# A Perceiver layer's cross-attention: the scores of a step's second 128 queries are issued after the first two turnings of probabilities

## The chip, the cores and the metric

The kernel runs on one core of one Trainium2 chip. The metric is device time in microseconds for one execution of the whole program. A core has a matrix engine (PE, with its weight loads listed apart as PEld), a vector engine (DVE), an activation engine (ACT), a general engine (POOL) and a queue for DMAs (SP). Each works through its own list of instructions in the order in which the program wrote them, and they meet through semaphores.

## What is computed

One layer of a Perceiver: x (2 x 256 x 256) attends to a context (2 x 4096 x 256) with 16 heads of 64, then come a self-attention and a gated feed-forward part with quantized weights. The change concerns the cross-attention alone:

```python
q = (scale * (Q @ Wq + bq)).reshape(bs, q_len, NH, DM)
k = (K @ Wk + bk).reshape(bs, kv_len, NH, DM)
v = (V @ Wv + bv).reshape(bs, kv_len, NH, DM)
qk = jnp.einsum('nlhd,nshd->nhls', q, k)
a = jax.nn.softmax(qk, axis=-1)
o = jnp.einsum('nhls,nshd->nlhd', a, v).reshape(bs, q_len, NH * DM)
return o @ Wo + bo
```

Q is the normalized x, K and V are both the context.

## The kernel before

The cross-attention is cut into 128 steps, n = 0 to 127. A step is one head (h), 1,024 of the 4,096 keys (chunk c) and all 256 queries of one batch, held as two halves of 128 (qt = 0 and 1). Sixteen steps (four chunks by four heads) make a group g, with k = n % 16; there are eight groups. Products are taken in a high and a low part for exactness, hence the names with hi and lo.

The matrix engine's list for step n is: the scores of the next step, n + 1 (`scores`, L292 to L305: for each half of the queries six matmuls with 64 rows, two at a time in the upper and lower half of the array, into that half's own two banks of `psS`); the wait of `bank_free` (L440 to L447), which holds the engine until the shared bank `psW` may be written again; in some steps one piece of other work into `psW`; two turnings of step n's probabilities (`turn`, four 128x128 transposes each, into `psT`); the projection of keys that will be needed four steps later (`project_k`, L341, into `psW`); the third and fourth turning; the products with the values (`values`, L329 and L330) with the projection of values (`project_v`, L354, into `psW`) between them. `project_k` has a wait of its own (L464 to L472) where the other work of the step has still to be read out of `psW`.

The other work depends on k. Steps with k = 1 to 7 of groups 1 to 7 turn outputs of the group before (`post`, L378), which DVE weighs (L667) out of `psW`; so does k = 0, where DVE first works out the weights (L652 to L659). Step k = 8 turns the summed outputs (`turn_o`, L386), k = 9 projects them (`project_o`, L395). Steps with k = 12 to 15 project queries of the next group (`project_q`, L365), which ACT (L533) and DVE (L630) read. Steps with k = 10 and 11 have nothing. Steps 0 to 7 and 48 to 63 also turn a piece of the context at their end (`turn_ctx`, L371) into `psW`, which ACT copies (L538) and DVE subtracts (L636, semaphore `prep_l`); the `bank_free` of the following step waits for that.

DVE's list in a step is: the maximum over the first half of the next step's scores (L613), the other work, `p_low` for the first two turnings (L619), the maximum over the second half, the sum of a weighed output (L676) if there is one, `p_low` for the last two, and the low part of the values (L624). ACT's list is: `p_high` twice (L544), the exponential of the first half (L510), the copy of the projected keys (L520), `p_high` twice, the exponential of the second half, the copies of values (L527) and outputs (L603). The order in which each engine's work is written out is the only thing that sets it; no planner is involved. The last four steps project no keys or values any more.

Of the kernel before, what the change touches and what calls it, by code (L numbers as in the profile page):

```python
# [14 lines left out]
def cross_attention(nc, x, ctx, Wq, bq, Wk, bk, Wv, bv, Wo, ident, y):  # L15
# [6 lines left out]
    QT = S // P  # L22
# [9 lines left out]
    N = GP * STEPS  # L32
# [12 lines left out]
    with ExitStack() as st:  # L45
# [79 lines left out]
        def wait(eng, s, val):  # L125
            if val > 0:
                eng.wait_ge(s, val)

        def place(n):

            return n // STEPS, n % STEPS // GH, n % GH

        def prep_unit(n):


            if n < 8:
                return 8 + n
            if (GP // 2 - 1) * STEPS <= n < GP // 2 * STEPS:
                return 2 * NP + n - (GP // 2 - 1) * STEPS
            return None  # L140
# [6 lines left out]
        def prob_slot(n, qt):  # L147
            return (2 * n + qt) % 3
# [140 lines left out]
        def _(pe):  # L289
            mm = pe.matmul  # L290

            def scores(n):  # L292
                g, c, h = place(n)
                if n % 2 == 0:
                    wait(pe, k_split, 4 * (n + 2))
                if c == 0:
                    wait(pe, q_ok, GH * g + h + 1)
                for qt in range(QT):
                    wait(pe, exp_ok, 2 * (n - 1) + qt + 1)
                    for i, (q, part) in enumerate(((q_hi, 0), (q_lo, 0), (q_hi, 1))):  # L300
                        for half in range(2):
                            rows = slice(HD * half, HD * half + HD)
                            last = mm(psS[:, qt, half * PIECE:(half + 1) * PIECE], q[rows, h, qt * P:(qt + 1) * P],  # L303
                                      kT[rows, n // 2 % KRING, h % 2, part, :], start=(i == 0), stop=(i == 2))
                    last.then_inc(s_ok, 1)  # L305

            def turn(n, t):
                if t == 0:
                    wait(pe, exp_ok, 2 * n + 2)
                wait(pe, pl_ok, 4 * n + t - 1)  # L310
                for k in range(2):
                    for qt in range(QT):
                        last = pe.transpose(psT[:, t % 2, k * S + qt * P:k * S + qt * P + P],  # L313
                                            prob[:, prob_slot(n, qt), (2 * t + k) * P:(2 * t + k + 1) * P],
                                            ident[:, :])
                last.then_inc(t_ok, 1)

            def values(n, t):
                h = n % GH
                unit = n // GH * GH + t  # L320
                wait(pe, pl_ok, 4 * n + t + 1)
                if t == 0:
                    wait(pe, oc_ok, n)
                if h == 0:
                    wait(pe, v_lo, unit + 1)
                for k in range(2):
                    w = v[:, unit % VRING, k, h, :, :].rearrange("p a d -> p (a d)")
                    at = (4 * n + t) % PRING
                    mm(psO[:, 0:S], w, pT_hi[:, at, k * S:(k + 1) * S], start=(t == 0 and k == 0), stop=False)  # L329
                    last = mm(psO[:, 0:S], w, pT_lo[:, at, k * S:(k + 1) * S], start=False,  # L330
                              stop=(t == TB - 1 and k == 1))
                last.then_inc(av_ok, 1)

            def project_k(m, dst):
                g, c, i = place(m)
                if m % STEPS == 0:
                    wait(pe, wk_ok, 2 * g + 2)
                piece = 2 * c + i % 2
                for j, (a, x_) in enumerate(((0, ctxT_hi), (1, ctxT_hi), (0, ctxT_lo))):
                    for kt in range(KT):  # L340
                        last = mm(dst, wk_s[:, a, kt, i // 2 * P:(i // 2 + 1) * P],  # L341
                                  x_[:, kt, piece * PIECE:(piece + 1) * PIECE],
                                  start=(j == 0 and kt == 0), stop=(j == 2 and kt == KT - 1))
                last.then_inc(k_ps, 1)
# [13 lines left out]
            def project_q(g, h, dst):  # L358
                if h == 0:
                    wait(pe, wq_ok, 8 * g + 8)  # L360
                b = g // QUADS
                for j, (a, x_) in enumerate(((0, xnT_hi), (1, xnT_hi), (0, xnT_lo))):
                    for kt in range(KT):
                        twin = wq_s[:, a, kt, h, :, :].rearrange("p a d -> p (a d)")
                        last = mm(dst, twin, x_[:, kt, b * S:(b + 1) * S],  # L365
                                  start=(j == 0 and kt == 0), stop=(j == 2 and kt == KT - 1))
                last.then_inc(q_ps, 1)
# [6 lines left out]
            def post(g, k, dst):  # L374
                h, qt = k // QT, k % QT
                wait(pe, oc_ok, STEPS * g + 12 + h + 1)
                for c in range(NCH):
                    last = pe.transpose(dst[:, c * P:(c + 1) * P], oT[:, h, out_slot(g, c), qt * P:(qt + 1) * P],  # L378
                                        ident[:, :])
                last.then_inc(post_ps, 1)  # L380

            def turn_o(g):
                wait(pe, comb, 16 * (g + 1))
                for half in range(2):
                    for qt in range(QT):
                        last = pe.transpose(psW[:, half * S + qt * P:half * S + (qt + 1) * P],  # L386
                                            on[:, qt, half * P:(half + 1) * P], ident[:, :])
                last.then_inc(o2_ps, 1)

            def project_o(g):  # L390
                wait(pe, wo_in, 16 * (g + 1))
                wait(pe, o2_ok, 2 * (g + 1))
                for qt in range(QT):
                    for half in range(2):
                        last = mm(psW[:, qt * D:(qt + 1) * D], o2T[:, half, qt * P:(qt + 1) * P], wo[:, half, :],  # L395
                                  start=(half == 0), stop=(half == 1))
                last.then_inc(y_ps, 1)
# [42 lines left out]
            def bank_free(n):  # L440

                if n == 0:
                    pe.wait_ge(q_ok, GH)
                elif prep_unit(n - 1) is not None:
                    wait(pe, prep_l, prep_unit(n - 1) + 1)
                else:
                    wait(pe, v_lo, min(n + LEAD, N))  # L447

            for n in range(N):
                g, k = n // STEPS, n % STEPS  # L450
                if n + 1 < N:
                    scores(n + 1)
                bank_free(n)
                if k < 8 and g >= 1:
                    post(g - 1, k, psW[:, :])
                elif k == 8 and g >= 1:
                    turn_o(g - 1)
                elif k == 9 and g >= 1:
                    project_o(g - 1)
                elif k >= 12 and g + 1 < GP:  # L460
                    project_q(g + 1, k - 12, psW[:, 0:S])
                turn(n, 0)
                turn(n, 1)
                if n + LEAD < N:  # L464
                    if k < 8 and g >= 1:
                        wait(pe, comb, 16 * (g - 1) + 2 * k + 1)
                    elif k == 8 and g >= 1:
                        wait(pe, o2_ok, 2 * g)
                    elif k == 9 and g >= 1:
                        wait(pe, y_ok, g)  # L470
                    elif k >= 12 and g + 1 < GP:
                        wait(pe, q_ok, GH * (g + 1) + k - 12 + 1)  # L472
                    project_k(n + LEAD, psW[:, :])
                turn(n, 2)
                turn(n, 3)
                early = prep_unit(n) is not None
                values(n, 0)
                if not early:
                    values(n, 1)
                if n + LEAD < N:  # L480
                    wait(pe, kraw_ok, n + LEAD + 1)
                    project_v(n + LEAD, psW[:, :])
                if early:
                    values(n, 1)
                values(n, 2)
                values(n, 3)
                u = prep_unit(n)
                if u is not None:
                    wait(pe, cst_in, 16 * (u // KT - FIRST + 1))
                    wait(pe, v_lo, n + LEAD + 1)  # L490
                    turn_ctx(u, cst, psW[:, :])
# [912 lines left out]
```

## Time and profile before

| | us |
|---|---|
| median of 3 runs | 1438.99 |
| lowest and highest | 1438.51, 1441.53 |
| the profiled execution | 1441.08 |
| its span in the trace | 1439.4 |
| PE busy | 1336.4 (93%) |
| DVE busy | 1025.7 (71%) |
| ACT busy | 882.1 (61%) |
| POOL busy | 621.7 (43%) |

The profiled execution took 1.7 us more than the span that its instructions cover. The scores of the cross-attention are computed from 42.6 us to 1200.8 us of the span, so the change touches four fifths of it. The records of a matmul overlap, since matmuls are pipelined; what counts here is where one matmul or weight load starts after the one before it.

### The profile page before, as it was taken

How to read it: one execution, taken by the hardware profiler on the slowest of the kernel's cores; microseconds unless marked ns; L12 is line 12 of the kernel's file. 1: busy time of each engine (PE TensorE's matmuls, PEld its weight loads, DVE VectorE, ACT ScalarE, POOL GpSimd, SP SyncE). 2: the span in 40 equal slices, each digit the busy share in tenths (PEclk: the TensorE clock that was granted, in tenths of full speed). 3: DMA queues.
4: the chain of work that ended last, by engine and by line, in shares of the span. 5: the costliest groups of instructions: out<-in, count | busy, mean ns of one | idle time of the engine just before them, and what ended most of it. 6: DMA issues, size and time to landing. Idle time of an engine off the chain costs nothing. (4 is left out here: it accounts for less than half of the span.)

```text
span 1439.4 us, 24781 instructions
## 1 busy us (share of the span) xinstructions
PE 1336.4 (93%) x9380; PEld 1136.4 (79%) x9380; DVE 1025.7 (71%) x1407; ACT 882.1 (61%) x1716; POOL 621.7 (43%) x749
## 2 busy tenths in 40 slices
PE   5899999999999999999999999999999997489857
PEld 4788888888888888888888888888888885267734
DVE  3666678767876786678766876687668867389666
ACT  2667666666666666766666666666666664256511
POOL 5355546454645454535454555455554440000000
PEclk9999999999999999999999999999999999589979
DMA  4010000000000010100000000000000000300000
GB/s 124 16 45 2 15 1 9 8 16 1 8 9 31 2 36 30 38 30 1 9 23 1 2 8 23 1 1 8 8 1 2 1 8 1 99 0 1 1 1 15
DMA packets 25940, 22.95 MB, mean 16 GB/s; under 512 B 5472, under 2 KB 25568, under 8 KB 25824
## 3 DMA queue, kind: packets, MB, share of 16 engines
q1 hardware_dynamic: 25824, 21.39, 5.0%
q8 instruction: 75, 1.23, 0.4%
q14 instruction: 41, 0.34, 0.1%
HBM read 20.86 MB, written 0.52 MB: 15 GB/s over the span
## 5 line engine op out<-in xcount | busy, mean ns | idle before, releaser
L544 ACT ACTIVATE pT_hi<-psT 128x512 fp32r<-128x512 f32 x512 | 293.1, 600 | 219.6 <-PE psT L313 199.2
L619 DVE TENSOR_TENSOR pT_lo<-psT,pT_hi 128x512 fp32r<-128x512 f32 x512 | 332.5, 685 | 81.6 <-ACT pT_hi L544 75.8
L613 DVE TENSOR_REDUCE negm<-psS 128x1 f32<-128x1024 f32 x256 | 311.7, 1218 | 52.3 <-PE psS L303 52.3
L264 POOL TENSOR_TENSOR kT<-kraw,khi 64x512 fp32r<-64x512 f32 x252 | 325.0, 1290 | 0.0
L258 POOL CAST khi<-kraw 128x512 fp32r<-128x512 f32 x126 | 76.9, 610 | 510.3 <-ACT kraw L520 509.5
L510 ACT ACTIVATE prob<-psS,negm 128x1024 f32<-128x1024 f32 x256 | 285.5, 1115 | 1.0 <-DVE negm L613 1.0
L313 PE MATMUL psT<-ident,prob 128*128 128x128 f32 x2048 | 268.5, 274 | 3.9 <-DVE pT_lo L619 3.9
L329 PE MATMUL psO<-pT_hi,v 128*128 128x256 f32 x1024 | 267.5, 294 | 1.2 <-DVE pT_lo L619 0.4
L313 PEld LDWEIGHTS psT<-ident,prob 128*128 128x128 f32 x2048 | 234.3, 141 | 34.0 <-issue 7.1
L330 PE MATMUL psO<-pT_lo,v 128*128 128x256 f32 x1024 | 255.7, 282 | 0.0
L303 PE MATMUL psS<-kT,q_hi 64*128 64x512 f32 x1024 | 194.6, 416 | 3.4 <-ACT prob L510 2.0
L329 PEld LDWEIGHTS psO<-pT_hi,v 128*128 128x128 f32 x1024 | 195.4, 191 | 2.7 <-DVE pT_lo L619 2.6
L330 PEld LDWEIGHTS psO<-pT_lo,v 128*128 128x128 f32 x1024 | 196.0, 191 | 0.0
L624 DVE TENSOR_TENSOR v<-psW,v 128x512 fp32r<-128x512 f32 x125 | 86.4, 691 | 115.7 <-ACT v L527 115.7
L354 PE MATMUL psW<-wv_s,ctxT_hi 128*128 128x256 f32 x1000 | 160.6, 283 | 0.0
L263 POOL CAST kT<-kraw 64x512 fp32r<-64x512 f32 x252 | 153.4, 609 | 15.6
L341 PE MATMUL psW<-ctxT_hi,wk_s 128*128 128x512 f32 x496 | 148.6, 421 | 10.7 <-DVE q_lo L630 5.9
L354 PEld LDWEIGHTS psW<-wv_s,ctxT_hi 128*128 128x128 f32 x1000 | 137.9, 192 | 0.1
L303 PEld LDWEIGHTS psS<-kT,q_hi 64*128 64x128 f32 x1024 | 96.2, 184 | 39.4 <-issue 6.4
L341 PEld LDWEIGHTS psW<-ctxT_hi,wk_s 128*128 128x128 f32 x496 | 83.8, 189 | 41.1 <-DVE q_lo L630 12.6
L303 PE MATMUL psS<-kT,q_lo 64*128 64x512 f32 x512 | 101.4, 393 | 0.0
L354 PE MATMUL psW<-wv_s,ctxT_lo 128*128 128x256 f32 x500 | 100.7, 283 | 0.0
(213 smaller groups left out, 1590.6 us busy)
## 6 DMA issues: line engine op xcount, KB each, us to landing
cst<-in_ctx_dram SPq DMA_DIRECT2D x12, 512.0 KB, 3.9
oT<-in_ctx_dram SPq DMA_DIRECT2D x4, 512.0 KB, 5.0
wraw<-in_L_xattn_Wk_dram SPq DMA_DIRECT2D x8, 256.0 KB, 2.6
wraw<-in_L_xattn_Wv_dram SPq DMA_DIRECT2D x8, 256.0 KB, 3.4
wraw<-in_L_xattn_Wq_dram SPq DMA_DIRECT2D x8, 256.0 KB, 2.6
wo<-in_L_xattn_Wo_dram SPq DMA_DIRECT2D x8, 256.0 KB, 2.7
ff_wdn<-in_L_ffn_w_down_dram SPq DMA_DIRECT2D x1, 704.0 KB, 8.7
ff_win<-in_L_ffn_w_gate_dram SPq DMA_DIRECT2D x1, 640.0 KB, 6.0
```

The source lines that it names most:

```text
L263: pool.tensor_copy(kT[half, m // 2 % KRING, h, 0, :], raw[own, :]).then_inc(k_split, 1)
L264: pool.tensor_tensor(kT[half, m // 2 % KRING, h, 1, :], raw[own, :], khi[own, :].bitcast(F32), ALU.subtract).then_inc(k_split, 1)
L303: last = mm(psS[:, qt, half * PIECE:(half + 1) * PIECE], q[rows, h, qt * P:(qt + 1) * P], kT[rows, n // 2 % KRING, h % 2, part, :], start= ...
L313: last = pe.transpose(psT[:, t % 2, k * S + qt * P:k * S + qt * P + P], prob[:, prob_slot(n, qt), (2 * t + k) * P:(2 * t + k + 1) * P], id ...
L329: mm(psO[:, 0:S], w, pT_hi[:, at, k * S:(k + 1) * S], start=(t == 0 and k == 0), stop=False)
L330: last = mm(psO[:, 0:S], w, pT_lo[:, at, k * S:(k + 1) * S], start=False, stop=(t == TB - 1 and k == 1))
L341: last = mm(dst, wk_s[:, a, kt, i // 2 * P:(i // 2 + 1) * P], x_[:, kt, piece * PIECE:(piece + 1) * PIECE], start=(j == 0 and kt == 0), st ...
L354: last = mm(dst[:, k * GD:(k + 1) * GD], x_[:, kt, keys], wv_s[:, a, kt, :], start=(j == 0 and kt == 0), stop=(j == 2 and kt == KT - 1))
L510: act.activation(prob[:, prob_slot(n, qt), :], psS[:, qt, :], ACT.Exp, bias=negm[:, g % 2, h, qt, c:c + 1], accum_out=lsum[:, g % 2, h, qt ...
L544: act.activation(pT_hi[:, i % PRING, :], psT[:, t % 2, :], ACT.Copy).then_inc(ph_ok, 1)
L613: dve.tensor_reduce(negm[:, g % 2, h, qt, c:c + 1], psS[:, qt, :], AX.X, ALU.max, negate=True)\
L619: dve.tensor_tensor(pT_lo[:, i % PRING, :], psT[:, t % 2, :], pT_hi[:, i % PRING, :].bitcast(F32), ALU.subtract).then_inc(pl_ok, 1)
```

## The change

`scores` takes a list of halves. A step calls it for the first half of the queries where it stood before, and for the second half after the second turning, ahead of `project_k` and of the wait in front of it. Nothing else is changed, on any engine; matmuls, tiles and semaphores are the same ones.

```diff
--- before.py
+++ after.py
@@ -289,13 +289,13 @@
         def _(pe):
             mm = pe.matmul
 
-            def scores(n):
+            def scores(n, qts=(0, 1)):
                 g, c, h = place(n)
                 if n % 2 == 0:
                     wait(pe, k_split, 4 * (n + 2))
                 if c == 0:
                     wait(pe, q_ok, GH * g + h + 1)
-                for qt in range(QT):
+                for qt in qts:
                     wait(pe, exp_ok, 2 * (n - 1) + qt + 1)
                     for i, (q, part) in enumerate(((q_hi, 0), (q_lo, 0), (q_hi, 1))):
                         for half in range(2):
@@ -449,7 +449,7 @@
             for n in range(N):
                 g, k = n // STEPS, n % STEPS
                 if n + 1 < N:
-                    scores(n + 1)
+                    scores(n + 1, (0,))
                 bank_free(n)
                 if k < 8 and g >= 1:
                     post(g - 1, k, psW[:, :])
@@ -461,6 +461,8 @@
                     project_q(g + 1, k - 12, psW[:, 0:S])
                 turn(n, 0)
                 turn(n, 1)
+                if n + 1 < N:
+                    scores(n + 1, (1,))
                 if n + LEAD < N:
                     if k < 8 and g >= 1:
                         wait(pe, comb, 16 * (g - 1) + 2 * k + 1)
```

On PE, at the start of step 1, a step without other work that follows one with a turned piece of context. `psS` holds scores, `psT` turned probabilities, `psW` is the shared bank; `exp_ok` says that an exponential has been taken, `pl_ok` that a turning has been read, `prep_l` that a context piece has left `psW`. Before:

```order
L303 MATMUL psS<-kT,q_hi 128x512
L303 MATMUL psS<-kT,q_lo 128x512 x2
L303 MATMUL psS<-kT,q_hi 128x512 x2
L303 MATMUL psS<-kT,q_hi 128x512 [waits exp_ok]
L303 MATMUL psS<-kT,q_hi 128x512
L303 MATMUL psS<-kT,q_lo 128x512 x2
L303 MATMUL psS<-kT,q_hi 128x512 x2
L313 MATMUL psT<-ident,prob 128x128 [waits pl_ok,exp_ok,prep_l]
L313 MATMUL psT<-ident,prob 128x128 x3
L313 MATMUL psT<-ident,prob 128x128 [waits pl_ok]
L313 MATMUL psT<-ident,prob 128x128 x3
L341 MATMUL psW<-ctxT_hi,wk_s 128x512 x4
```

After:

```order
L303 MATMUL psS<-kT,q_hi 128x512
L303 MATMUL psS<-kT,q_lo 128x512 x2
L303 MATMUL psS<-kT,q_hi 128x512 x2
L313 MATMUL psT<-ident,prob 128x128 [waits pl_ok,exp_ok,prep_l]
L313 MATMUL psT<-ident,prob 128x128 x3
L313 MATMUL psT<-ident,prob 128x128 [waits pl_ok]
L313 MATMUL psT<-ident,prob 128x128 x3
L303 MATMUL psS<-kT,q_hi 128x512 [waits exp_ok,q_ok,k_split]
L303 MATMUL psS<-kT,q_hi 128x512
L303 MATMUL psS<-kT,q_lo 128x512 x2
L303 MATMUL psS<-kT,q_hi 128x512 x2
L341 MATMUL psW<-ctxT_hi,wk_s 128x512 x4
```

The second half's six matmuls (four rows) moved behind eight transposes, and the transposes, with their wait for `prep_l`, moved up by those six.

On PE again, in step 13, which projects queries (L365) whose reading out of `psW` (`q_ok`) the first matmul of L341 waits for. Before:

```order
L303 MATMUL psS<-kT,q_hi 128x512 [waits exp_ok]
L303 MATMUL psS<-kT,q_hi 128x512
L303 MATMUL psS<-kT,q_lo 128x512 x2
L303 MATMUL psS<-kT,q_hi 128x512 x2
L365 MATMUL psW<-xnT_hi,wq_s 128x256 [waits v_lo]
L365 MATMUL psW<-xnT_hi,wq_s 128x256 x3
L365 MATMUL psW<-xnT_lo,wq_s 128x256 x2
L313 MATMUL psT<-ident,prob 128x128 [waits pl_ok,exp_ok]
L313 MATMUL psT<-ident,prob 128x128 x3
L313 MATMUL psT<-ident,prob 128x128 [waits pl_ok]
L313 MATMUL psT<-ident,prob 128x128 x3
L341 MATMUL psW<-ctxT_hi,wk_s 128x512 [waits q_ok]
```

After:

```order
L365 MATMUL psW<-xnT_hi,wq_s 128x256 [waits v_lo]
L365 MATMUL psW<-xnT_hi,wq_s 128x256 x3
L365 MATMUL psW<-xnT_lo,wq_s 128x256 x2
L313 MATMUL psT<-ident,prob 128x128 [waits pl_ok,exp_ok]
L313 MATMUL psT<-ident,prob 128x128 x3
L313 MATMUL psT<-ident,prob 128x128 [waits pl_ok]
L313 MATMUL psT<-ident,prob 128x128 x3
L303 MATMUL psS<-kT,q_hi 128x512 [waits exp_ok,k_split]
L303 MATMUL psS<-kT,q_hi 128x512
L303 MATMUL psS<-kT,q_lo 128x512 x2
L303 MATMUL psS<-kT,q_hi 128x512 x2
L341 MATMUL psW<-ctxT_hi,wk_s 128x512 [waits q_ok]
```

Here the second half's scores now stand between the turnings and the matmul that waits for `q_ok`; the projection of queries follows the first half's scores directly.

## Rows read from the trace of the kernel before

**Rows 1.** Windows: stretch, length, busy us (instructions) by engine, PE clock, DMA, GB/s.
```profile
787.00:1190.00 403.00, 398.28 (x2946) 345.90 (x2944) 301.90 (x389) 270.62 (x507) 208.58 (x246) 1.00 0.02 6
```
**Rows 2.** Timeline of a step without other work: start, length, engine, line, work.
```profile
740.84 0.28 PE L330 MATMUL psO<-pT_lo,v 128*128 128x256 f32 x1
741.04 0.18 PEld L303 LDWEIGHTS psS<-kT,q_hi 64*128 64x128 f32 x2
...
741.15 0.19 PEld L303 LDWEIGHTS psS<-kT,q_lo 64*128 64x128 f32 x2
741.38 0.40 PE L303 MATMUL psS<-kT,q_lo 64*128 64x512 f32 x2
...
742.31 0.39 PE L303 MATMUL psS<-kT,q_hi 64*128 64x512 f32 x2
742.63 0.85 PEld L313 LDWEIGHTS psT<-ident,prob 128*128 128x128 f32 x8 [0.36 <-issue]
...
743.45 0.76 PEld L341 LDWEIGHTS psW<-ctxT_hi,wk_s 128*128 128x128 f32 x4
...
749.27 0.50 PE L303 MATMUL psS<-kT,q_hi 64*128 64x512 f32 x2
```
**Rows 3.** Timeline of a step that turns outputs, PE and DVE.
```profile
704.61 0.69 DVE L624 TENSOR_TENSOR v<-psW,v 128x512 fp32r<-128x512 f32 x1 [0.68 <-ACT v L527]
...
704.83 0.50 PE L303 MATMUL psS<-kT,q_hi 64*128 64x512 f32 x2
...
705.84 1.23 DVE L613 TENSOR_REDUCE negm<-psS 128x1 f32<-128x1024 f32 x1 [0.53 <-PE psS L303]
...
706.91 1.04 PE L313 MATMUL psT<-ident,prob 128*128 128x128 f32 x8
...
707.11 0.69 DVE L667 TENSOR_TENSOR oweighed<-psW,wts 128x512 f32<-128x512 f32 x1
...
707.85 1.20 PE L341 MATMUL psW<-ctxT_hi,wk_s 128*128 128x512 f32 x4
```
**Rows 4.** Timeline of a group's first step, where DVE works out weights beforehand.
```profile
790.78 0.50 PE L341 MATMUL psW<-ctxT_hi,wk_s 128*128 128x512 f32 x1 [0.57 <-DVE oweighed L667]
```
**Rows 5.** Timeline of a step that projects queries.
```profile
758.74 0.50 PE L303 MATMUL psS<-kT,q_hi 64*128 64x512 f32 x2
...
760.33 0.53 PEld L365 LDWEIGHTS psW<-xnT_hi,wq_s 128*128 128x128 f32 x4 [0.36 <-issue]
...
761.14 1.03 PE L313 MATMUL psT<-ident,prob 128*128 128x128 f32 x8
761.34 0.47 ACT L533 ACTIVATE q_hi<-psW,bqT 128x256 fp32r<-128x256 f32 x1 [2.10 <-PE psW L365]
...
761.85 0.48 DVE L630 SCALAR_TENSOR_TENSOR q_lo<-psW,bqT,q_hi 128x256 fp32r<-128x256 f32 x1 [0.87 <-ACT q_hi L533]
762.38 0.30 PEld L341 LDWEIGHTS psW<-ctxT_hi,wk_s 128*128 128x128 f32 x2 [0.45 <-DVE q_lo L630]
```
**Rows 6.** Timeline after a turned piece of context: a step without other work.
```profile
591.45 0.63 PE L371 MATMUL psW<-ident,cst 128*128 128x128 f32 x4 [0.28 <-DVE v L624]
592.00 0.19 PEld L303 LDWEIGHTS psS<-kT,q_hi 64*128 64x128 f32 x2 [0.17 <-issue]
...
592.74 0.69 DVE L636 TENSOR_TENSOR ctxT_lo<-psW,ctxT_hi 128x512 fp32r<-128x512 f32 x1 [1.44 <-ACT ctxT_hi L538]
...
593.59 0.85 PEld L313 LDWEIGHTS psT<-ident,prob 128*128 128x128 f32 x8 [0.36 <-DVE ctxT_lo L636]
...
594.41 0.77 PEld L341 LDWEIGHTS psW<-ctxT_hi,wk_s 128*128 128x128 f32 x4
```
**Rows 7.** The same after a turned piece, in a step that turns outputs.
```profile
502.08 0.19 PEld L303 LDWEIGHTS psS<-kT,q_hi 64*128 64x128 f32 x2 [0.17 <-issue]
...
505.29 0.30 PEld L341 LDWEIGHTS psW<-ctxT_hi,wk_s 128*128 128x128 f32 x2 [0.34 <-DVE oweighed L667]
```
**Rows 8.** Timeline of step 124, the first without projections.
```profile
1184.41 0.50 PE L303 MATMUL psS<-kT,q_hi 64*128 64x512 f32 x2
...
1187.32 1.29 DVE L619 TENSOR_TENSOR pT_lo<-psT,pT_hi 128x512 fp32r<-128x512 f32 x2 [0.68 <-ACT pT_hi L544]
...
1190.39 0.39 PE L329 MATMUL psO<-pT_hi,v 128*128 128x256 f32 x1
```

## Prediction

> **What bounds the kernel now.** I read the share of busy time by stretch first. Over 403 us of steps PE has work in flight for 398 us, at the full granted clock, with DVE at 302 and ACT at 271 [rows 1]. So PE sets the pace, and the question is what its list costs in another order. For that I read the timeline of one step of each kind, by starts. The reader is to see two sorts of lost PE time: places where the array is not fed although nothing is waited for, and places where PE waits before the projection of keys (L341).
>
> The first sort stands at both edges of the block of scores [rows 2]. The last value matmul starts at 740.84; inside that block they follow each other every 0.12, so the array is free at 740.96, yet the scores' first weight load starts at 741.04: 0.08 lost. The second pair's load starts at 741.15, so the first load held things up for 0.11 with no matmul to cover it. Then pairs start every 0.23 (the second at 741.38, the last at 742.31), and the last one leaves the array free at 742.54, but the transposes' load starts at 742.63: 0.09 lost. The whole block takes 1.59 from its first load to the next work's. Loads of other work don't show this: from the transposes to L341 it is 743.45 right at the end of eight starts of 0.11. The same 1.59 stands before L365 [rows 5], and when the scores follow transposes of the context (591.45 to 592.00 for four, where four need 0.44 and the first one's load 0.05) about 0.06 is again lost at entry [rows 6]. What differs at all these edges is that scores use 64 rows of the array and everything else 128.
>
> **What the change adds.** A second block of three pairs, between transposes and L341: 0.08 at entry, 0.11 for its first load, 0.09 at its exit, and 0.11 for the first load of L341, now without cover. That is **0.39 a step** if PE waits for nothing. One block of three pairs takes 1.59 - 3 x 0.23 = 0.90 to the next work's load. I take 0.39 from these rows; the bounds are 0.34 and 0.44 (the entry at 0.06 rather than 0.08 and the uncovered load of L341 a little shorter, against a longer exit).
>
> The Trainium skill (TensorEngine Tiling (Array Packing), Key Properties) says that changing the tiling mode drains the engine. The gaps of 0.08 and 0.09 agree with that; the two uncovered loads are more than the sentence says.
>
> **What it removes**, by kind of step. Times in brackets count from the step's first load of scores. In the new order other work starts at 0.90, the turnings after it, they take 0.87 (eight starts of 0.11; 0.92 when they come straight after scores), the second block starts 0.08 later, and L341's load 0.90 after that.
>
> - Steps with nothing else, 15 and the opening one: no wait before L341 to cover, so +0.39 each: **+6.2**.
> - Steps that turn outputs [rows 3]: L341 waits for the weighing, which ends at 707.80, and starts at (3.02). The weighing follows the maximum of the first half, 705.84 to 707.07, which doesn't move. In the new order the turnings start at (1.39) instead of 706.91 (2.08), end at (2.26), and L341 can start at (2.34 + 0.90 = 3.24). So the wait vanishes and +0.22 is left. There are 42 of them outside the stretch below, and six steps with the output projection, whose L341 waits about as long: 48 x 0.22 = **+10.5**. The six that turn summed outputs wait a little longer: **+0.4** together.
> - The first step of a group [rows 4]: the weighing is released at 3.68 after the start, later than 3.24, so L341 starts as before: **0**, six times.
> - Steps that project queries [rows 5]: L341 waits for the low part of the queries until 762.38 (3.64). In the new order they are projected at (0.90) instead of 760.33; their reading ends at about (2.9), set by DVE's maximum; turnings run (1.71) to (2.58), and L341 can start at (3.56): -0.08 each, 24 times: **-2.0**.
> - The last three steps with scores [rows 8]: no L341 follows, and the chain of readings binds. The second maximum starts after the readings of the first two turnings, 1187.32 to 1188.61, and the values' third part waits until 1190.39. Turnings that start 0.69 earlier move the chain by about 0.65, since the first maximum ends at (2.24) and lets the readings start at (2.27) rather than 1187.32 (2.91): **-2.0** together.
>
> **What it uncovers.** After a step that ended with a turned piece of context, the bank is busy until DVE has read it at 592.74 + 0.69 = 593.43 (1.43), and the turnings wait for that [rows 6]. Before, 1.59 of scores hid it fully: the load starts at 593.59, right when scores end. With 0.90 of scores it is not hidden, and PE waits 0.58 until (1.48). It gets back only 0.11 of its former 1.59. For the ten such steps without other work the turnings then end at (2.40), and L341's load starts at (3.38) instead of 594.41 (2.41), its matmul 0.01 later still: +0.98, **+9.8**. Four such steps project queries: from (1.48) the sum gives (4.14) instead of (3.64): **+2.0**. Ten have other work; for those that turn outputs it gives 1.48 + 0.49 + 0.87 + 0.08 + 0.90 = (3.82) instead of 505.29 (3.21) [rows 7]: about +0.61, **+6.2**.
>
> All waits of other engines behind this have room. DVE's second maximum finds its scores about 1.0 after the block's start, (3.4) in a step that turns outputs, while its own reading of the turnings keeps it busy until (4.2). The bank is free of values at 705.30 (0.47) [rows 3], before the (0.90) at which other work wants it. The third and fourth turning come later than before while what they wait for comes earlier. POOL's split keys and the DMAs are asked for at the same places of the list.
>
> **The sum:** 6.2 + 10.5 + 0.4 - 2.0 - 2.0 + 9.8 + 2.0 + 6.2 = **+31.1 us**. On the profiled execution's own 1441.1 (span 1439.4 and 1.7 around it) that is 1472.2; it lies 2.1 above the median of 1438.99, so against the median I say **1470.1**. With 0.05 more or less for a change of tiling in some 118 steps: 1464 to 1476.
>
> **Rivals.**
>
> 1. *The changes of tiling cost nothing in the new place.* For it: the transposes are short, and weight loads elsewhere hide. Against: the entry from context transposes and the exits above. With 0 instead of 0.39, the plain steps cost nothing, those that turn outputs stay at the weighing, the 24 with queries gain 0.47 each (-11.3), the last three 2.0, and the uncovered steps still add 10 x 0.59, 4 x 0.11 and 10 x 0.22: 8.5. Sum -4.8: **1434**, on the faster side. It decides from about 0.07 a step downwards.
> 2. *The drain is paid but both loads are hidden*: 0.17 a step. 16 x 0.17 - 24 x 0.30 - 2.0 + 10 x 0.76 + 4 x 0.28 + 10 x 0.39 = +6: **1445**. The Trainium skill (TensorE: Matmul & The Clock Gate, Step-by-step: what each phase is for) has the engine pull weight loads ahead of running matmuls when row groups don't conflict or a background buffer is used; by that rule this is the outcome. Inside a block of scores the trace agrees, at its edges it doesn't.
> 3. *The uncovering does not happen*, because the piece of context is read sooner than DVE's row shows: 24 x 0.58 = 14 less, **1456**.
> 4. *The waits aren't covered*: if what releases L341 moves along with it, all 127 steps pay 0.39 and the uncovering comes on top: 49.5 + 14 = +64, **1503**. Against it: the maximum of the first half, which sets the weighing, stays.
> 5. *No effect*, because the engine would take matmuls in another order than written: **1439**.
>
> **Chances.** Forecast 0.76, rival 1 0.04, rival 2 0.05, rival 3 0.05, rival 4 0.08, rival 5 0.02. The range reaches down to rival 3 and, with the forecast's own bounds and a few us by which the clock may fall differently in the part after the steps, up to 1484: **1456 to 1484**. A measurement can tell about 0.2% (3 us) from no change. Faster: 0.04; within 0.2%: 0.03 (rival 5 and a share of the others' edges); slower: 0.93.
>
> **What would show it.** In the new profile: a plain step of 8.62 instead of 749.27 - 741.04 = 8.23; two blocks of three pairs of scores, each 0.90 to the next load; no wait of L341 for L667 or L630 except at a group's first step; steps of about 10.1 after a turned piece, with PE waiting about 0.58 for L636 before the turnings. Blocks of 0.7 would point to rivals 1 and 2; a PE wait for L619 or L510, or DVE's second maximum idle for scores, would mean that a chain I called loose is not.

## The result and the profile after

The changed kernel takes 1472.97 us (median of 4 runs, 1471.44 to 1474.92); the kernel before, measured again beside it, 1440.26. The ratio is 1.0221, with a 95% interval of 1.0189 to 1.0253: slower by about 32 us. Forecast were 1470.1 us and 31.1 us more. The span grew from 1439.4 to 1469.7 us.

The page shows why shares of busy time don't help here: PE is busy for 93% before and after.

```profile
span 1469.7 us, 24860 instructions
...
PE 1364.8 (93%) x9380; PEld 1126.9 (77%) x9380; DVE 1029.4 (70%) x1407; ACT 892.2 (61%) x1716; POOL 621.7 (42%) x749
```

Lines behind the added call are two higher in the new kernel (L613 is L615, L636 is L638, L667 is L669). The timeline of a step without other work, which answers to [rows 2]:

```profile
766.91 0.28 PE L330 MATMUL psO<-pT_lo,v 128*128 128x256 f32 x1
767.12 0.19 PEld L303 LDWEIGHTS psS<-kT,q_hi 64*128 64x128 f32 x2
...
767.69 0.39 PE L303 MATMUL psS<-kT,q_hi 64*128 64x512 f32 x2
768.01 0.86 PEld L313 LDWEIGHTS psT<-ident,prob 128*128 128x128 f32 x8 [0.36 <-DVE v L626]
...
769.03 0.19 PEld L303 LDWEIGHTS psS<-kT,q_hi 64*128 64x128 f32 x2 [0.17 <-issue]
...
769.14 0.19 PEld L303 LDWEIGHTS psS<-kT,q_lo 64*128 64x128 f32 x2
...
769.60 0.40 PE L303 MATMUL psS<-kT,q_hi 64*128 64x512 f32 x2
...
769.92 0.77 PEld L341 LDWEIGHTS psW<-ctxT_hi,wk_s 128*128 128x128 f32 x4 [0.36 <-issue]
```

There are two blocks of three pairs, each 0.89 from its first load to the load of the next work (767.12 to 768.01, 769.03 to 769.92). The second one has everything that the old block had at its edges. Its second pair's load comes 0.11 after the first, so the first load was not covered. The last pair starts at 769.60 and leaves the array at 769.83, and the next load waits until 769.92.

After a turned piece of context, to be read beside [rows 6]:

```profile
612.16 0.19 PEld L303 LDWEIGHTS psS<-kT,q_hi 64*128 64x128 f32 x2 [0.17 <-issue]
...
612.90 0.69 DVE L638 TENSOR_TENSOR ctxT_lo<-psW,ctxT_hi 128x512 fp32r<-128x512 f32 x1 [1.44 <-ACT ctxT_hi L540]
...
613.64 0.86 PEld L313 LDWEIGHTS psT<-ident,prob 128*128 128x128 f32 x8 [0.96 <-DVE ctxT_lo L638]
...
615.56 0.30 PEld L341 LDWEIGHTS psW<-ctxT_hi,wk_s 128*128 128x128 f32 x2 [0.36 <-issue]
```

DVE reads the piece until 613.59, at the same distance from the step's start as before (1.43), and the turnings start at 1.48. Before, no time was lost there. Two entries of the table of waits (who waited for whom: us in total, times, longest) have grown. Before:

```profile
PEld psT L313 <- DVE ctxT_lo L636: 3.6, 10, 0.4
PEld psW L378 <- DVE ctxT_lo L636: 2.9, 8, 0.4
```

After:

```profile
PEld psT L313 <- DVE ctxT_lo L638: 9.6, 10, 1.0
...
PEld psW L378 <- DVE ctxT_lo L638: 7.8, 8, 1.1
```

These entries count the idle time of the weight loads from the end of the last load, 0.36 each before, when PE lost nothing. What counts is the growth: 0.60 and 0.61 a time.

And a step that turns outputs, beside [rows 3]:

```profile
831.84 0.50 PE L303 MATMUL psS<-kT,q_hi 64*128 64x512 f32 x2
...
832.85 1.22 DVE L615 TENSOR_REDUCE negm<-psS 128x1 f32<-128x1024 f32 x1 [0.53 <-PE psS L303]
...
833.99 0.68 DVE L669 TENSOR_TENSOR oweighed<-psW,wts 128x512 f32<-128x512 f32 x1
...
835.09 0.30 PEld L341 LDWEIGHTS psW<-ctxT_hi,wk_s 128*128 128x128 f32 x2 [0.36 <-DVE oweighed L669]
```

The weighing ends at 834.67 (2.83), and L341 could only start at 3.25: the wait is covered, as forecast, and the row's "<-DVE oweighed" names a semaphore that had come 0.42 earlier. The weighing itself started at 2.15, not at 2.28 as before, though the maximum in front of it runs from 1.01 to 2.23 in both traces. The prediction had not foreseen that.

Step lengths from the two traces, from one step's first scores to the next's:

| kind of step | number | before | after | measured change, sum | forecast, sum |
|---|---|---|---|---|---|
| no other work, and the opening step | 16 | 8.23 (opening 14.67) | 8.63 (14.89) | +6.2 | +6.2 |
| outputs turned, output projected | 48 | 8.86, 10.18 | 9.06, 10.40 | +9.7 | +10.5 |
| summed outputs turned | 6 | 8.99 | 9.06 | +0.4 | +0.4 |
| first of a group | 6 | 9.68 | 9.68 | 0.0 | 0 |
| queries projected | 24 | 9.46 | 9.39 | -1.7 | -2.0 |
| after a piece, no other work | 10 | 9.04 | 10.03 | +9.9 | +9.8 |
| after a piece, queries projected | 4 | 10.35 | 10.88 | +2.1 | +2.0 |
| after a piece, others | 10 | 9.17 to 11.08 | 9.80 to 11.88 | +6.5 | +6.2 |
| two of the last three | 2 | 7.54 | 6.84 | -1.4 | -1.3 |
| **all of them** | 126 | 1156.9 | 1188.9 | **+31.9** | **+31.8** |

The rest of the span, from step 126 on, got 1.3 us shorter; 0.7 of it is that last step with scores, and 0.6 lies in the part that the change doesn't touch, where the granted clock was a little higher (last section).

### The profile page after: what moved, and what is told of

Same layout as the page of the kernel before. It is cut to its first block and busy times, and to the rows that moved or that the text cites. A ratio compares the mean times of both kernels' runs of the same rounds, so it can differ in the third digit from the quotient of the medians.

```text
span 1469.7 us, 24860 instructions
## 1 busy us (share of the span) xinstructions
PE 1364.8 (93%) x9380; PEld 1126.9 (77%) x9380; DVE 1029.4 (70%) x1407; ACT 892.2 (61%) x1716; POOL 621.7 (42%) x749
## 5 line engine op out<-in xcount | busy, mean ns | idle before, releaser
L621 DVE TENSOR_TENSOR pT_lo<-psT,pT_hi 128x512 fp32r<-128x512 f32 x512 | 340.4, 687 | 109.4 <-ACT pT_hi L546 90.2
L615 DVE TENSOR_REDUCE negm<-psS 128x1 f32<-128x1024 f32 x256 | 311.6, 1218 | 52.5 <-PE psS L303 52.5
L264 POOL TENSOR_TENSOR kT<-kraw,khi 64x512 fp32r<-64x512 f32 x252 | 324.3, 1287 | 0.0
L303 PE MATMUL psS<-kT,q_hi 64*128 64x512 f32 x1024 | 228.6, 443 | 3.3 <-ACT prob L512 2.0
L341 PE MATMUL psW<-ctxT_hi,wk_s 128*128 128x512 f32 x496 | 148.4, 420 | 2.4 <-DVE oweighed L669 2.4
L522 ACT ACTIVATE kraw<-psW,bkT 128x512 f32<-128x512 f32 x124 | 85.3, 688 | 95.1 <-PE psW L341 87.2
L341 PEld LDWEIGHTS psW<-ctxT_hi,wk_s 128*128 128x128 f32 x496 | 83.6, 188 | 59.7 <-issue 28.1
```

The costliest lines, as they stand in the source:

```text
L264: pool.tensor_tensor(kT[half, m // 2 % KRING, h, 1, :], raw[own, :], khi[own, :].bitcast(F32), ALU.subtract).then_inc(k_split, 1)
L615: dve.tensor_reduce(negm[:, g % 2, h, qt, c:c + 1], psS[:, qt, :], AX.X, ALU.max, negate=True)\
L621: dve.tensor_tensor(pT_lo[:, i % PRING, :], psT[:, t % 2, :], pT_hi[:, i % PRING, :].bitcast(F32), ALU.subtract).then_inc(pl_ok, 1)
```

## The experiments

The theory: the second block of scores costs by its edges, where the array goes from 128 rows to 64 and back, and the earlier turnings meet a bank that is still being read. The rivals: the block costs by something else than its rows, or the time after a context piece is DVE's, not the bank's. The kernel before, run beside them, had a median of 1442.88 us (7 runs) for the first four experiments and 1440.39 (17 runs) for the last four; each ratio is against its own.

**The scores whole again after a context piece.**

```diff
-                    scores(n + 1, (0,))
+                    piece = n > 0 and prep_unit(n - 1) is not None
+                    scores(n + 1, (0, 1) if piece else (0,))
...
-                if n + 1 < N:
+                if n + 1 < N and not piece:
                     scores(n + 1, (1,))
```

> The changed kernel, but in the 24 steps that follow a turned piece of context the scores of both halves are taken together again, as before. Theory (a change of tiling costs 0.39 a step, and the piece's way out of the shared bank, 1.48 after the step's start, is hidden by 1.59 of scores and not by 0.90): the 24 steps return to their lengths of before, 10 x 1.00 + 14 x about 0.6 = 18.6 us less than the changed kernel, so +13 to +14 us against the kernel before: 1454. Rival (there is no uncovered wait, only changes of tiling): 24 x 0.39 = 9.4 us less, 1463. In the trace PE should not wait for L638 any more.

1452.71 us, ratio to the kernel before 1.0067 (1.0044 to 1.0090). All 24 steps have their old lengths within 0.04, and the sum over the steps is 13.4 us above before instead of 31.9. The 18.5 us are twice what changes of tiling alone would give (24 x 0.39 = 9.4), so the uncovered wait is real and half of this part.

**The wait for the bank moved to its first writer.**

```diff
+                other = (k < 10 and g >= 1) or (k >= 12 and g + 1 < GP)
+                if other:
+                    bank_free(n)
-                bank_free(n)
...
                     scores(n + 1, (1,))
+                if not other:
+                    bank_free(n)
```

> The changed kernel, with the wait for the shared bank moved in steps without other work from the front of the turnings to the front of the projection of keys, which is the first to write that bank there. Theory: in the ten such steps after a turned piece the turnings start 0.89 after the step's start instead of 1.48, and the steps take 9.53 instead of 10.12: 5.9 us less than the changed kernel, 1467 (+26 against before). Rival (the late thing in these steps is DVE's maximum, which also comes after the piece, and not the bank): no change, 1473. The other steps should not move.

1465.09 us, ratio 1.0157 (1.0129 to 1.0184). The timeline after a context piece:

```profile
605.96 0.19 PEld L303 LDWEIGHTS psS<-kT,q_hi 64*128 64x128 f32 x2 [0.17 <-issue]
...
606.70 0.69 DVE L642 TENSOR_TENSOR ctxT_lo<-psW,ctxT_hi 128x512 fp32r<-128x512 f32 x1 [1.44 <-ACT ctxT_hi L544]
606.86 0.86 PEld L313 LDWEIGHTS psT<-ident,prob 128*128 128x128 f32 x8 [0.36 <-issue]
```

The turnings start 0.90 after the step, while DVE is still at the piece, and these ten steps take 9.44 on average instead of 10.03. The other 14 with a piece before them don't move. The ten steps give 5.9 us, as expected; over all steps it is 6.2 us less than the changed kernel, as the opening step also got 0.2 shorter. DVE's maximum starts at 1.35 in both kernels and costs nothing, so that rival is out.

**The second block over 128 rows.**

```diff
+                    if qt == 1 and qts == (1,):
+                        for i, (q, part, half) in enumerate(((q_hi, 0, 0), (q_hi, 0, 1), (q_lo, 0, 1))):
+                            last = mm(psS[:, qt, half * PIECE:(half + 1) * PIECE], q[:, h, qt * P:(qt + 1) * P],
+                                      kT[:, n // 2 % KRING, h % 2, part, :], start=(i < 2), stop=(i != 1))
+                        last.then_inc(s_ok, 1)
+                        continue
```

> The changed kernel, but the second half's scores are three matmuls over all 128 rows instead of three pairs over 64 rows each, so they sum the wrong products: the two key halves are added up, and one low-part product is left out. The array's time is the same, 3 x 0.23. Theory (the cost lies in the change between 64 and 128 rows: 0.08 and 0.09 of gaps, 0.11 and 0.11 of loads that nothing covers): the block takes 0.69 and no gap stands around it, so 0.39 less in every step in which PE waits for nothing; by the sum made before with 0 in place of 0.39, about 5 us below the kernel before, 1435 to 1438. Rival (a block of its own costs this much whatever its rows, by its semaphores or because the bank changes): 1473 as the changed kernel.

1426.78 us, ratio 0.9895 (0.9869 to 0.9922): the cost of the split is gone, and more. The timeline (L319 are the turnings, L302 the second block, L347 the keys):

```profile
740.25 0.86 PEld L319 LDWEIGHTS psT<-ident,prob 128*128 128x128 f32 x8 [0.36 <-DVE v L632]
...
741.07 0.30 PEld L302 LDWEIGHTS psS<-kT,q_hi 128*128 128x128 f32 x2
741.10 0.71 PE L302 MATMUL psS<-kT,q_hi 128*128 128x512 f32 x2
...
741.65 0.40 PE L302 MATMUL psS<-kT,q_lo 128*128 128x512 f32 x1
741.65 0.89 PEld L347 LDWEIGHTS psW<-ctxT_hi,wk_s 128*128 128x128 f32 x4
741.88 1.08 PE L347 MATMUL psW<-ctxT_hi,wk_s 128*128 128x512 f32 x4
```

L347's first load starts with the block's last matmul, at 741.65, and its matmul follows at 741.88, 0.23 later, with no gap. The block has the same place, the same semaphores and the same banks; the rows of the array are what differs, and with them the pairing, the operands and the number of matmuls (three instead of six). A step without other work takes 8.23, exactly as before the change. This is the step of the prediction that carried most, and it holds.

The steps together are 13.0 us shorter than before, where about 5 had been expected. The 42 steps that turn outputs were expected to stay as they were, and got 6.7 us shorter together: they come out at 8.70, below the 8.86 of before. The expectation kept L341's load at 3.02; in this run it starts at 2.88, since the weighing starts at 2.15 here too. What had held the weighing until 2.28 before is in the row of PE that belongs to [rows 3]:

```profile
706.41 0.66 PE L378 MATMUL psW<-ident,oT 128*128 128x128 f32 x4
```

The last transpose of outputs ends at 707.07 (2.24), and the weighing follows 0.04 later. The maximum ends at 707.07 too, but it had not been the one to wait for: in the changed kernel and in this run the weighing starts 0.08 before the record of the maximum ends. With the transposes over at 1.55, the maximum alone sets it. The twelve steps that turn or project the summed outputs got 3.1 us shorter for the same reason: what L341 waits for there is released by PE's own work, which now comes earlier. Against these 9.8 us stands 1.0 that the steps with queries gained less than expected.

**The second block between the first and the second turning.**

```diff
                 turn(n, 0)
-                turn(n, 1)
                 if n + 1 < N:
                     scores(n + 1, (1,))
+                turn(n, 1)
```

> The changed kernel, with the second half's scores between the first and the second turning, so that transposes follow them and not the projection of keys. Same number of changes of tiling. Theory (the first load after a change is uncovered, and it holds things up for 0.055 before a transpose and for 0.11 before the projection of keys): 0.055 less in about 115 steps, 6 us less than the changed kernel, 1467; if the second reading comes too late for the values' last part in steps that turn outputs, a part of that is lost. Rival (what costs is the number of edges alone): 1473, no change.

1470.22 us, ratio 1.0196 (1.0170 to 1.0223). Timeline:

```profile
765.79 0.50 PE L303 MATMUL psS<-kT,q_hi 64*128 64x512 f32 x2
...
766.68 0.66 PE L313 MATMUL psT<-ident,prob 128*128 128x128 f32 x4
767.07 0.53 PEld L341 LDWEIGHTS psW<-ctxT_hi,wk_s 128*128 128x128 f32 x3
767.10 0.70 PE L341 MATMUL psW<-ctxT_hi,wk_s 128*128 128x512 f32 x2
```

The load of L341 is covered by a transpose again. Steps without other work take 8.56 instead of 8.63, those with queries 9.32 instead of 9.39, those that turn outputs 9.01 instead of 9.06: 0.05 to 0.07 a step, near the 0.055 expected. Given back is 1.9 us in the first steps of groups (10.00 instead of 9.68) and 1.8 in the last two, where the second turning comes later and DVE's reading of it with it. In the first steps of groups it is not the turning. There L341 still waits for the weighing, and a small operation of DVE in front of the weighing ends with one of POOL, 0.32 later than in the changed kernel (1.14 long instead of 0.82; last section):

```profile
810.34 1.29 POOL L264 TENSOR_TENSOR kT<-kraw,khi 64x512 fp32r<-64x512 f32 x1
810.54 1.14 DVE L654 TENSOR_TENSOR le<-edif,lsum 128x32 f32<-128x32 f32 x1
```

Over the steps it is 3.6 us less than the changed kernel. The medians alone, 2.8 us apart, could not have told this from nothing; the step lengths do.

**One more trip to 64 rows and back.**

```diff
                 turn(n, 0)
+                if n + 1 < N:
+                    scores(n + 1, (1,), (0, 1))
                 turn(n, 1)
                 if n + 1 < N:
-                    scores(n + 1, (1,))
+                    scores(n + 1, (1,), (2,))
```

The last argument of `scores`, added here, is the list of pairs that it issues; the semaphore is raised with the third.

> The changed kernel with one more change of tiling to 64 rows and back: of the second half's three pairs, two stand between the first and the second turning and the third after the second. Theory (each return trip costs 0.08 + 0.11 + 0.09 and the first uncovered load behind it, 0.055 before transposes): about 0.34 more in each step in which PE waits for nothing and in nearly all of the others, about 118 x 0.34 = 40 us more than the changed kernel: 1510. Rival (the cost comes once with the order, not by edges): 1473.

1517.68 us, ratio 1.0525 (1.0502 to 1.0547). Timeline (L316 turnings, L305 scores, L344 keys):

```profile
792.71 0.19 PEld L305 LDWEIGHTS psS<-kT,q_hi 64*128 64x128 f32 x2 [0.17 <-issue]
...
793.37 0.42 PEld L316 LDWEIGHTS psT<-ident,prob 128*128 128x128 f32 x4 [0.36 <-issue]
...
793.96 0.19 PEld L305 LDWEIGHTS psS<-kT,q_hi 64*128 64x128 f32 x2 [0.17 <-issue]
...
794.39 0.75 PEld L344 LDWEIGHTS psW<-ctxT_hi,wk_s 128*128 128x128 f32 x4 [0.24 <-issue]
```

A block of one pair still takes 0.43 for 0.23 of array time. Steps without other work take 8.95 (+0.32 on the changed kernel), steps that turn outputs 9.41 (+0.35), all steps together 41.4 us more, where 40 had been expected. So the price is paid for each trip.

**The split only where it pays.**

```diff
-                    scores(n + 1)
+                    split = n >= N - LEAD or (k >= 12 and g + 1 < GP and prep_unit(n - 1) is None)
+                    scores(n + 1, (0,) if split else (0, 1))
...
+                if n + 1 < N and split:
+                    scores(n + 1, (1,))
```

> The kernel before, with the two halves taken apart only in the 24 steps that project queries and follow no turned piece of context, and in the last three steps with scores. Theory (there the second block of scores covers a wait that is longer than its changes of tiling cost, and in the last steps the turnings' earlier start shortens the chain of readings): 24 x 0.07 + 3 x 0.7 = 3.8 us less than before, 1436 to 1437 on a scale where before is 1440. Rival (a step's gain is given back in the next, since the chains of ACT and DVE stay as long): 1440.

1435.52 us against 1440.39, ratio 0.9971 (0.9956 to 0.9986); the steps are 3.7 us shorter. Nothing is given back.

**Queries into the other half of psO.** The matmuls of the values write 256 of the 512 columns of their bank; the projected queries can go into the others, with waits so that no two engines are in that bank at once. ACT and DVE read them there.

```diff
-                    project_q(g + 1, k - 12, psW[:, 0:S])
+                    wait(pe, oc_ok, n)
+                    project_q(g + 1, k - 12, psO[:, S:2 * S])
...
-                    elif k >= 12 and g + 1 < GP:
-                        wait(pe, q_ok, GH * (g + 1) + k - 12 + 1)
...
+                if k >= 12 and g + 1 < GP:
+                    wait(pe, q_ok, GH * (g + 1) + k - 12 + 1)
                 values(n, 0)
```

> The kernel before, scores together, with the projection of queries written to the unused half of the values' bank psO instead of the shared bank psW, so that the projection of keys has no reading to wait for. Theory (what the second block of scores covers in these steps is 0.41 of PE time lost before L341, and nothing is late behind it): 28 x 0.41 = 11.5 us less than before, 1428 to 1429. Rival (the readings of the turnings, which come after DVE's q_lo, are late next, so the third and fourth turning wait instead): 1435 to 1440, with PE idle before the turnings at L313.

1432.95 us, ratio 0.9935 (0.9917 to 0.9953). In the timeline DVE reads the queries while L341 runs, where before L341 waited for it [rows 5]:

```profile
763.19 0.48 DVE L631 SCALAR_TENSOR_TENSOR q_lo<-psO,bqT,q_hi 128x256 fp32r<-128x256 f32 x1 [0.88 <-ACT q_hi L534]
763.25 0.53 PEld L341 LDWEIGHTS psW<-ctxT_hi,wk_s 128*128 128x128 f32 x3
```

The 28 steps gain 12.3 us, 11.5 had been expected, and the turnings wait for nothing new. The steps as a whole are 11.5 us shorter: six of the seven first steps of a group lost 0.33 to 0.40 each (last section), and others gained a little. The interval of the medians allows 7 to 12 us. In this profile the part behind the steps took 243.6 us against 239.8 before, nearly all of it where nothing was changed (last section).

**The three things together.** On the kernel before: queries in psO, the split in the last three steps alone, and

```diff
+                if k == STEPS - 1:
+                    weigh_end(g)
                 if n + LEAD < N:
                     v_low(n + LEAD, psW[:, :])
...
-                if k == STEPS - 1:
-                    weigh_end(g)
```

> The kernel before with three things: queries projected into psO as in the run before, the halves taken apart in the last three steps with scores alone, and DVE's weights of a group (L652 to L659 of the kernel before) worked out ahead of the last low part of the values, in a time in which DVE waits, so that the first maximum of the next step isn't pushed back. Theory: 11.5 + 2.1 + 7 x 0.6 = 17.8 us less than before: 1422. Rival (what DVE does earlier delays the low part of the values, and with it the shared bank, so the third item gives nothing): 1426.

**1419.91 us**, ratio 0.9851 (0.9834 to 0.9868), the fastest of all. Not all of the 20.5 us between the medians is the edit's own. In the traces the steps are 18.1 us shorter than before (17.8 had been expected) and the last step with scores 0.7; another 2.0 lie in the part that nothing changes, at a higher granted clock (0.86 against 0.83). In the first step of a group, which answers to [rows 4]:

```profile
1063.49 0.69 DVE L670 TENSOR_TENSOR oweighed<-psW,wts 128x512 f32<-128x512 f32 x1
...
1064.24 0.53 PEld L341 LDWEIGHTS psW<-ctxT_hi,wk_s 128*128 128x128 f32 x3
```

L341 starts 3.02 after the step's start, as in other steps that turn outputs. These steps take 9.00 instead of 9.68.

## Why the prediction was right

*The block and its edges.* 0.39 a step was forecast from the old block's edges; 0.40 was measured (8.63 against 8.23). The 128-row run shows that it goes with the change of rows (and of the pairing that comes with it), the run with a third block that it is paid per trip. The run with the block between the turnings shows that the uncovered load behind the block is a part of its own, which shrinks by 0.05 to 0.07 when a transpose follows. The Trainium skill's sentence (TensorEngine Tiling (Array Packing), Key Properties), that changing the tiling mode drains the engine, agrees with this case; the drain by itself is 0.08 to 0.09 at each edge here, and the two uncovered loads (0.11 each) more than double it. Why the loads are not pulled ahead at an edge, no run tells: they might be held by the drain, or by the rows that they go to.

*What the block covers.* Every kind of step came out within 0.05 us of the forecast, the first of a group at exactly zero. The largest miss in the sum is in the steps that turn outputs: 0.20 a step instead of 0.22, because 35 of the 42 had been 8.87 and not 8.83 long before. That L341's wait for DVE or ACT would go, and that nothing would be late behind it, is in the rows of PE: only edges stand before L341 now, except at a group's first step.

*What it uncovers.* Forecast 18.0 for 24 steps, measured 18.5. The 0.58 of waiting and its releaser came out as read from one row of DVE and the length of a half block. Two experiments separate it from the edges: 18.5 us for edges and waits in the 24 steps, and 5.9 us for ten of the waits alone.

*How good the number is.* The forecast's 31.1 counts the last step with scores; the traces give 31.9 - 0.7 = 31.2. An agreement to 0.1 is partly luck: 0.8 too much for the steps that turn outputs is made up by 0.6 too little after a piece and 0.3 too much gain in the steps with queries.

*What was wrong.* The reading "the weighing follows the maximum of the first half", and with it rival 1's price. It left the steps that turn outputs at the weighing's old time and gave 1434 for a second block without edges; the run gave 1427. The maximum indeed doesn't move, but what released the weighing at 2.28 was the end of the outputs' transposes, which the change moves from 2.24 to 1.55. In the forecast itself this was hidden, as L341 starts at 3.25, later than the weighing's end by either reading (2.97 or 2.83). Two smaller readings were loose as well. The 3.68 of [rows 4] is L341's start; the weighing ends 0.05 before it. And 743.45 is 0.82 after 742.63, less than eight starts of 0.11: L341's load starts before its turn among the matmuls, which only supports that loads are covered there.

Rivals 2 to 5 fell: loads are uncovered, the wait is there, L341's waits are covered, and PE keeps the written order.

## What to carry to other kernels

When an engine bounds a kernel and its work is cut in two, the edges of the existing block are already in the trace, and they say what a second block will cost. When work is moved later to cover one wait, ask what it covered at its old place: here a bank that another engine was reading until 1.43 had been hidden by 1.59 of scores. And where a wait is to be filled, first ask whether it has to exist: other columns of a bank and another place in DVE's list made the steps some 16 us shorter, where filling the waits made them 32 longer. And when two things end together in a row, ask what would happen if one of them moved.

## What the runs showed of the hardware

*DVE and POOL.* One small operation of DVE, with both inputs in SBUF, ends when POOL's own ends, not when its 128x32 elements are done. In the kernel before, and in the run with queries in psO:

```profile
786.97 1.29 POOL L264 TENSOR_TENSOR kT<-kraw,khi 64x512 fp32r<-64x512 f32 x1
787.49 0.82 DVE L652 TENSOR_TENSOR le<-edif,lsum 128x32 f32<-128x32 f32 x1
```

```profile
1065.05 1.29 POOL L264 TENSOR_TENSOR kT<-kraw,khi 64x512 fp32r<-64x512 f32 x1
1065.22 1.17 DVE L653 TENSOR_TENSOR le<-edif,lsum 128x32 f32<-128x32 f32 x1
...
1069.06 0.30 PEld L341 LDWEIGHTS psW<-ctxT_hi,wk_s 128*128 128x128 f32 x2 [1.35 <-DVE oweighed L668]
```

POOL ends at 788.26 and 1066.34, DVE at 788.31 and 1066.39. The last group's, with POOL done, takes 0.18. In the ten traces this operation starts 68 times while POOL's L264 is running, and each time it ends 0.05 after it, whatever it takes (0.81 to 1.17). POOL's place relative to DVE shifted by 0.35 when the steps with queries got shorter, and PE lost as much in six of the seven first steps of a group. The seventh, step 64, is the exception that tells most:

```profile
634.63 0.19 DVE L653 TENSOR_TENSOR le<-edif,lsum 128x32 f32<-128x32 f32 x1
634.74 1.27 POOL L264 TENSOR_TENSOR kT<-kraw,khi 64x512 fp32r<-64x512 f32 x1
634.86 0.19 DVE L655 TENSOR_REDUCE L<-le 128x8 f32<-128x32 f32 x1
635.08 0.20 DVE L657 RECIPROCAL rL<-L 128x8 f32<-128x8 f32 x1
635.31 0.74 DVE L660 TENSOR_TENSOR wts<-edif,rL 128x32 f32<-128x32 f32 x1
```

Here DVE's operation starts 0.11 before POOL's and takes 0.19. The two that follow have one input each and run beside POOL in 0.19 and 0.20. The next with two inputs takes 0.74 (0.19 without POOL) and ends 0.04 after POOL. Step 64 of the run with the block between the turnings shows the same order and the same 0.18 and 0.74. The Trainium skill (GPSIMD Engine Reference, Specifications) lists contention over SBUF for DVE instructions with two SBUF inputs; these rows agree. No run took POOL's operation away, so the cause is read from the order of the starts and the coincidence of the ends.

*The clock behind the steps.* Windows of the part that no run changes, from the first outputs turned after the last step to the end, in the kernel before, the changed one and the run with queries in psO (stretch, length, busy us by engine, the granted clock as a share, DMA, GB/s):

```profile
1212.70:1439.40 226.70, 167.14 (x810) 123.29 (x808) 153.60 (x265) 79.92 (x218) 1.50 (x6) 0.83 0.07 19
```

```profile
1243.70:1469.70 226.00, 166.27 (x810) 122.73 (x808) 153.53 (x265) 79.97 (x218) 1.50 (x6) 0.85 0.07 19
```

```profile
1200.60:1431.00 230.40, 170.85 (x810) 126.83 (x808) 153.78 (x265) 79.67 (x218) 1.50 (x6) 0.81 0.06 18
```

The instructions are the same ones, and the clock there moves between its two levels, 1.2 and 2.4 GHz. With a mean share of 0.83, 0.85 and 0.81 the part takes 226.7, 226.0 and 230.4 us. Over the ten traces it lies between 224.6 and 230.8 us, and the two longest go with the lowest shares. Runs of one kernel spread alike: the kernel before took 1438.6 us at a mean clock of 0.973 over the whole run and 1445.4 at 0.964. So a few us between two profiles, or two medians, of this program can be clock, and step lengths taken from the traces tell more.
